# Streaming 17 instead of 32 columns per head in the class query's product with the values

## The reference

```
h = relu(x W0) * (x W1) Wo                      # per token
h = concat([cls_tok, h])                        # 513 rows: the class token is row 0
h = h + attention(layernorm(h))                 # 16 heads of 16, softmax over 513 keys,
                                                # inputs and weights of the projections quantised
h = h + experts(layernorm(h))                   # 8 experts, the best two of each token
```

## Time and profile before

| | |
|---|---|
| median of three executions | 2512.09 us (2507.2 to 2514.85) |
| the profiled execution | 2501.11 us |
| its span, first to last instruction | 2499.2 us |
| token phase | up to about 1706 us |
| between the phases | about 1706 to 1823 us |
| expert phase | about 1823 us to the end |
| PE busy | 2160.9 us (86%) |
| DVE busy | 1521.1 us (61%) |
| ACT busy | 1203.2 us (48%) |
| POOL busy | 965.7 us (39%) |
| granted clock of PE, mean | 0.934 of full speed |

### The profile page before, as it was taken

How to read it: one execution, slowest core, us unless ns; L and a number is a source line. 1 busy time by engine, 2 the same in 40 slices (tenths; PEclk the granted TensorE clock), 3 DMA queues, 4 the chain that set the end, 5 groups by cost and what they waited for, 6 DMA issues and landing times. The chain is left out here.

```text
span 2499.2 us, 46805 instructions
## 1 busy us (share of the span) xinstructions
PE 2160.9 (86%) x12048; PEld 1071.8 (43%) x12049; DVE 1521.1 (61%) x4004; ACT 1203.2 (48%) x2360; POOL 965.7 (39%) x894
## 2 busy tenths in 40 slices
PE   4889989899898998988989888984069999999998
PEld 2433434443433433443344333322036666666665
DVE  3477877777766786777777778763453333333332
ACT  1256656455554565555555556551233444444443
POOL 2323343342333433344343343232335555555554
PEclk9899999999998998999999999886589999999999
DMA  2322232222222222222222122201433333333332
GB/s 96 80 81 61 72 90 69 73 69 82 78 67 67 69 81 70 79 63 77 74 77 81 52 82 79 75 10 34 152 85 56 54 55 53 54 54 53 54 53 39
DMA packets 181070, 171.96 MB, mean 69 GB/s; under 512 B 40002, under 2 KB 169620, under 8 KB 180884
## 3 DMA queue, kind: packets, MB, share of 16 engines
q1 hardware_dynamic: 150612, 134.94, 18.1%
q0 software_dynamic: 30272, 34.80, 8.9%
HBM read 100.82 MB, written 68.93 MB: 68 GB/s over the span
## 5 line engine op out<-in xcount | busy, mean ns | idle before, releaser
L1141 DVE TENSOR_REDUCE mxs<-bank 128x1 f32<-128x512 f32 x1024 | 698.0, 686 | 342.0 <-PE bank L491 272.0
L817 ACT ACTIVATE pt<-bank 128x512 f32<-128x512 f32 x1024 | 584.2, 593 | 369.7 <-PE bank L500 354.0
L491 PE MATMUL bank<-ks,qs 96*128 96x512 bf16 x1024 | 410.1, 401 | 74.5 <-DVE mxs L1141 53.0
L500 PE MATMUL bank<-qs,ks 99*128 99x512 bf16 x1024 | 405.7, 397 | 6.6 <-ACT pt L817 5.5
L1688 POOL DMA_INDIRECT out<-y_sb,ids x136 | 215.4, 1584 | 273.9 <-DMA out<-y_sb,ids 208.8
L509 PE MATMUL bank<-pt,v_sb 128*32 128x512 f32 x2048 | 288.6, 635 | 0.0
L491 PEld LDWEIGHTS bank<-ks,qs 96*128 96x128 bf16 x1024 | 104.7, 102 | 334.9 <-DVE mxs L1141 169.8
L985 POOL TENSOR_TENSOR cadd<-vcls,pr 128x256 f32<-128x256 f32 x64 | 40.5, 634 | 500.2 <-DVE pr L1188 498.5
L1813 DVE TENSOR_TENSOR hid_e<-bank,act_g 128x512 f32<-128x512 f32 x136 | 94.1, 692 | 211.8 <-PE bank L1734 211.8
L1817 DVE TENSOR_TENSOR hl<-bank,hh 128x512 bf16<-128x512 f32 x136 | 94.1, 692 | 211.2 <-ACT hh L1787 211.2
L1734 PE MATMUL bank<-gu_h,xh 128*128 x544 | 208.0, 382 | 12.6 <-issue 8.8
(11 more groups left out here) (281 smaller groups left out, 3499.8 us busy)
## 6 DMA issues: line engine op xcount, KB each, us to landing
qs<-qk_dram SPq DMA_DIRECT2D x128, 128.0 KB, 2.4
ks<-qk_dram SPq DMA_DIRECT2D x64, 192.0 KB, 3.1
xt<-x_t SPq DMA_DIRECT2D x16, 512.0 KB, 3.9
h_dram<-h_sb SPq DMA_DIRECT2D x16, 512.0 KB, 2.8
qs<-qk_dram SPq DMA_DIRECT2D x128, 64.0 KB, 2.1
ks<-qk_dram SPq DMA_DIRECT2D x64, 128.0 KB, 3.0
hw<-h_dram SPq DMA_DIRECT2D x16, 512.0 KB, 4.2
out<-hw SPq DMA_DIRECT2D x16, 512.0 KB, 2.9
```

What stands on the lines that cost most here:

```text
L491: mm(score[u % 2][:, :], qs[0:QK, h, blk(t)], ks[0:QK, h, :], start=True, stop=True) \
L500: mm(scoret[u % 2][:, :], ks[0:QK + MROWS, h, blk(t)], qs[0:QK + MROWS, h, :], start=True, stop=True).then_inc(s("pe_st"), 1)
L817: f(pt[:, t % 2, j, :], scoret[u % 2][:, :], ACT.Exp).then_inc(s("act_exp"), 1)
L1141: v.reduce_max(mxs[:, t, g * GH + j:g * GH + j + 1], score[u % 2][:, :], AX.X).then_inc(s("dve_mx"), 1)
```

## The change

The product in slot 34 streams only the 17 used columns of each head: 16 heads times 17 are 272 columns where there were 512. The moving side is then no longer one contiguous run per partition but 16 runs of 17 f32, 32 apart. The result stands packed in the first 272 columns of `d2`. The mask is read with the same steps (17 of each 32), `pvd` is kept packed with 17 columns per head, and the gathering product in slot 42 streams 68 columns where there were 128. The number of instructions, their order on each engine and what they wait for are as before. The sizes of `v_sb` and `vcls` are too.

```
+VC = HD + 1
...
-    diagonal = cst[:, C_DG:C_DG + NH * VW]
+    diagonal = cst[:, C_DG:C_DG + NH * VW].rearrange("p (h w) -> p h w", h=NH)[:, :, 0:VC]
+    used = lambda ap: ap.rearrange("p (h w) -> p h w", w=VC)
...
-    pvd = sb("pvd", [128, NH * VW])
+    pvd = sb("pvd", [128, NH, VC])
...
                         for t in range(TB):
-                            last = mm(d2[VW * t:VW * (t + 1), :], pc[:, W.par, t, :],
-                                      v_sb[:, W.par, t, :, :].rearrange("p h w -> p (h w)"), start=True, stop=(t > 0))
+                            last = mm(d2[VW * t:VW * (t + 1), 0:NH * VC], pc[:, W.par, t, :],
+                                      v_sb[:, W.par, t, :, 0:VC], start=True, stop=(t > 0))
                             if t == 0:
-                                mm(d2[0:VW, :], pc[0:1, W.par, TB, :], vcls[0:1, W.par, :, :].rearrange("p h w -> p (h w)"),
+                                mm(d2[0:VW, 0:NH * VC], pc[0:1, W.par, TB, :], vcls[0:1, W.par, :, 0:VC],
                                    start=False, stop=True)
...
                         for k in range(NG):
-                            last = mm(d2[0:NG, 0:GH * VW], cst[:, C_SEL + k * NG:C_SEL + (k + 1) * NG],
-                                      pvd[:, k * GH * VW:(k + 1) * GH * VW], start=(k == 0), stop=(k == NG - 1))
+                            last = mm(d2[0:NG, 0:GH * VC], cst[:, C_SEL + k * NG:C_SEL + (k + 1) * NG],
+                                      pvd[:, heads(k), :], start=(k == 0), stop=(k == NG - 1))
...
-                        v.tensor_tensor(pvd[:, :], d2[:, :], diagonal, ALU.mult).then_inc(s("dve_pvd"), 1)
+                        v.tensor_tensor(pvd[:, :, :], used(d2[:, 0:NH * VC]), diagonal, ALU.mult).then_inc(s("dve_pvd"), 1)
...
-                        got = d2[0:NG, 0:128].rearrange("p (j w) -> p j w", w=VW)
+                        got = used(d2[0:NG, 0:GH * VC])
```

## The result

On the chip that timed the two together, the changed kernel took 2473.55 us (median of four runs, 2469.88 to 2480.26) and the kernel before 2509.64 us (four runs, 2506.43 to 2514.85). The ratio is 0.9857, with a 95% interval of 0.9826 to 0.9889, so 36 us less (28 to 44 by the interval). The forecast was 21 us less and 2491 us. The measured time lies 2.5 us under the range. The direction was right, the size was not.

The account below looks back on a forecast made before the run. PE was taken to set the pace before DVE's busy stretch in each image's slot 34; per-image gains summed to 18.7 to 22.3 us, taken as 21, so 2512.1 - 21 = 2491 us, range 2476 to 2509 (8 in 10).

Parts of the forecast that it names:

- What bounds the kernel, and where the gain goes: Token phase, slot 34: PE sets the pace before 427.89 us, DVE after; the whole 1.20 us gain is passed on.
- the three idle times: DVE's waits for PE's score tiles behind slot 34's product: 1.61, 2.06, 0.89 us become 0.4, about 2.3, 0.9.
- The product, 1.20 us an image: Slot 34: three rounds of passes shrink from 0.98 to 0.58 us each at full clock, saving 1.20 us an image.
- the 2.40 of the text: Slot 34's product at half clock: the columns taken away are worth double, 2.40 us an image.
- The steps at nothing: Slot 34's stepped reads of the moving side cost what contiguous columns cost; taken as no price.
- The bound on the other side: Slot 34's steps so dear that 272 columns cost what 512 did, taking away the 1.20 us.
- Gathering and mask at nothing: Slot 42's gathering (0 to 0.40 us) and DVE's mask (0.25 us) are hidden by waits, so counted as nothing.
- The sum: Whole kernel: images' gains add to 22.3 us, or 18.7 with every product at full clock; 21 taken.
- Images 14 to 16: Last images: 14 gains only the mask's 0.25 us, 15 at half clock 2.4, the last about 1.6 with gathering.
- the clock's falls about as many as now: Forecast case for PE's clock over the kernel: gain passed on, falls unchanged; chance 0.58, range 2484 to 2499 us.
- clock kinder: Rival, PE's clock in the image loop: long images become short, time around 2479 us or below; chance 0.11.
- number of half-clock products: Slot 34: three of 16 products at half clock; leaving three would put the size off with the mechanism right.

Follow-up runs that it names:

- contiguous: Changed kernel, but slot 34's product streams 272 adjacent columns of a weight in place of the values; 2445.25 us against 2455.11 for the kernel before, ratio 0.9924.
- cols24: Changed kernel with 24 of 32 columns a head instead of 17 in product, mask and gathering; 2442.14 us against 2458.01 for the kernel before, ratio 0.9960.
- every_fourth: Changed kernel, but the four key tiles' product streams 272 columns with a step of four f32; 2453.85 us against 2455.87 for the kernel before, ratio 0.9987.
- after_again3: The changed kernel without an edit, timed again on chip B2; 2443.31 us against 2455.11 for the kernel before, ratio 0.9931.
- before_again: The kernel before without an edit, timed again on chip A2; 2510.25 us against 2511.53 for the kernel before, ratio 1.0002.
- warm_after: Changed kernel plus 20 unread filler matmuls on PE ahead of line 647 in slot 55; 2446.41 us against 2455.11 for the kernel before, ratio 0.9956.

## Why the prediction was wrong in size

**What bounds the kernel, and where the gain goes.** Right. PE sets the pace in front of 427.89 in the earlier trace rows, and the three idle times changed as forecast.

**The product, 1.20 us an image.** Right at full clock, 1.18 to 1.19 us. At half clock also: 5.55 us became 3.15, the 2.40 of the text.

**The steps at nothing.** Right; contiguous and cols24 show it. The bound on the other side was real for another pattern, every_fourth.

**Gathering and mask at nothing.** The mask was hidden, the gathering was not: this is the first step that failed. "PE would only wait at line 784 for 1.0 instead of 0.6 us" assumed that DVE was busy by itself up to `oc`. Between the gathering and `oc` lies another score tile for which DVE waits 0.51 us. It gave 0.40 us an image up to `oc` where line 1251 was short, 0.13 us where POOL lengthened it, over 14 images 2 to 6 us.

**The sum.** With that term the 18.7 to 22.3 us of the text become 21 to 28, and the runs gave 23 to 26 at one clock. 21 was 2 to 5 us short.

**Images 14 to 16.** The rows at full clock give these differences from the product's start to the ranks: in image 14 15.57 us before and 15.16 in after_again3, 0.41 for the 0.25 of the text; in image 15 15.48 in before_again and 13.90, 1.58; in the last 7.92 and, in warm_after, 6.38, 1.54 for the 1.6. From the fourteenth product to the sixteenth the two profiles on A1 take 156.5 and 151.2 us, but with other clocks, so no term can be read from it.

**The clock.** This is the second step that failed, and probably the larger miss: of the 15 us between 21 and 36, the gathering has 2 to 5 and about 9 are left for the clock. The forecast's case was "the clock's falls about as many as now", a term of zero, and the rival "clock kinder" had 0.11 and stood at 2479. The runs put the term at +7 to +10 us on B1 to B3, at -4.5 us on A2, where its interval reaches zero, and at about -9 us on A1, which is inferred. So the same change costs clock on one kind of chip and does not on the other; that it gives clock back there is likely, not shown. It is luck of the chip, too, on which side the 21 us missed: on the B chips the medians lay only 12 to 17 us apart, and 21 would have been too much. The prediction had seen falls of 5 us an image in the earlier trace rows, and gave them a chance for getting worse, but no spread in the forecast itself. A term of ±10 us around the centre would have put the range's lower end near 2466 instead of 2476.

**The other signs.** The text named the number of half-clock products as what could put the size off. It went from three of 16 to seven (images 3, 4, 5, 10, 13, 14 and 16, most of them only in part at half clock), and yet the kernel was faster than forecast and its mean clock .935 against .934. So that number does not stand for the clock's cost. The expert phase kept its time: from its first pass of `gu_l` with `xh` to the end of the span it took 666.0 us, against 666.2. The absolute forecast stood on a median of 2512.09 us; the median of before beside the result was 2509.64, which is 2 of the 17 us.

What stays open is why the clock falls with the change on one kind of chip and not on the other. That the stall at slot 54 separates them is seen; that it is the cause was not tried, as no filler kernel met a chip with it.

## What to carry to other kernels

Price a shorter matmul by its columns and rounds, then look at each later place where its neighbour engine waits for the next tile: a gain counts as nothing only if no such wait lies before the point that sets the end, and rows that join two instructions hide one. Where PE's granted clock moves between runs, fit time against clock over all runs and compare kernels at one clock; here this turned differences of 12 to 36 us into 23 to 26. For the forecast, give the clock a term of its own with both signs.

## What the runs showed of the hardware

- A mean granted clock lower by 0.001 over the kernel goes with 1.86 us more, and its changes make up three quarters of the variance between runs of one kernel on one chip (7.0 us of deviation without it, 3.5 with it).
- Sixteen runs of 17 f32 columns stream as fast as 272 adjacent ones (0.58 us a round); 272 single columns with a step of four take 1.05 us at full clock and 1.05 to 1.09 us at half, where the runs of 17 take 1.04 to 1.06.
- A DVE operation on 128x4 that starts within 0.03 us of one of POOL took 0.63 us in 171 of 180 images, with POOL's at 0.63. In the other nine it took 0.16 us and POOL's 0.67.
- Three chips lack a stall of 4 us in most images at slot 54 that A1 and A2 have (ACT's 44.7 us of remote waits on A1). The same kernel takes 55 us more there, 30 of them at one clock.
- Four f32 matmuls of 32 output partitions each run side by side when they follow each other (1.18 us for the five products); with a pass for the partitions of the first between it and the others, it took 1.76 us.
